# Scan layer and expert tiles: first weights of the last stage into other buffers, and ScalarE's evictions re-ordered

## Chip, cores and metric

One core of a Trainium2 chip runs the whole program. The metric is the device time of one execution in microseconds: the median of three executions of the kernel before is 1581.85 us (1579.13 to 1584.12).

## The reference

`x` is 8 sequences of 512 tokens with 256 features, all float32. A small block computes six modulation vectors for each sequence from `c`. Then:

```
h = layernorm(x) * (1 + ca) + sa
x = x + ga * mamba(h)              # scan layer
h = layernorm(x) * (1 + cb) + sb
x = x + gb * ffn(h)                # 8 experts, 2 for each token

mamba(h):  xi, z = split(rmsnorm(h) @ W_in)          # 512 channels each
           xc = silu(conv(xi)); dt, B, C = split(xc @ W_x)
           dt = softplus(dt @ W_dt + b_dt)
           state = exp(dt * A) * state + dt * xc * B  # 16 states per channel, over 512 tokens
           y = (sum over states of state * C + D * xc) * silu(z)
           return y @ W_out
ffn(h):    scores = h @ Wg; the two best experts of 8, weights by softmax
           out_e = relu((layernorm(h) * gamma_e + beta_e) @ W1_e + b1_e) @ W2_e + b2_e + h
           return the weighted sum of the two
```

`W1` is 256 x 1024 for each expert and `W2` 1024 x 256, 1 MB each in float32. The layernorm ahead of gamma and beta is the same for all experts.

## The kernel before, in words

**The loop.** A body n (0 to 7) runs one sequence through the scan. Its 16 steps s are the 16 states, and each step has four chunks of 128 channels (128 partitions x 512 tokens), so that there are 8 x 16 x 4 = 512 units. For each unit ScalarE computes the decay exp(dt * A) into one of two places in PSUM (`decays`, L1124), GpSimd the input dt * xc * B into a ring of nine tiles `dBu` (L873), and VectorE the scan (L1965), whose result goes over the input. When the four scans of a step are done, TensorE transposes its states in four tiles (`states`, L1477). Two of them VectorE multiplies by C and adds to `y` (L1976), two ScalarE multiplies into `hc` (`times_c`, L1108), and TensorE sums these with the identity (`add_up`, L1486). VectorE is a step ahead of these: it runs scan 0, a product with C, scan 1, scan 2, a product with C, scan 3. A decay waits until the scan two units before has freed its place: this is the "scan ring" (`DA_RING` of 2).

**What rides in the loop.** Between the units of body n lie the preparation of sequence n + 1 (in ScalarE's queue: `norm`, `conv_in`, `softplus_in` and `softplus_exp` at L1091 to 1096, which read the dt product of TensorE at L1466, and `z_in`), and what comes behind the scan for sequence n - 1 (`o_norm` and `o_xhat`, the normalisations of the second half of the layer at L1012; `scores_in`; `top_exp`; `count_in`, L1155, which copies the counts of tokens for each expert that TensorE sums at L1569 to 1573). The order is written out by hand, engine by engine, in one function `body` for each: what stands between `decays(..., (1,))` and `decays(..., (2,))` is run in that place in every body for which its condition holds.

**Tokens by expert.** The output of the second normalisation goes to a table of rows in HBM (`rows_d`, written by GpSimd's indirect transfers, `send_rows`, L791), sorted by expert. A tile is 128 such rows of one expert. Tiles 0 to 11 are computed inside bodies 3 to 7: their W1 and W2 come in halves of 0.5 MB ("pieces") into slots. Slots 0, 1 and 2 lie in `wp` (`expert_pieces` in the profile), slots 3 and 4 are the two halves of `win`, which first held the input weights. TensorE computes them in `tile_h` (L1621) and `tile_y` (L1634), ScalarE evicts the first product with bias and relu in `tile_hin` (L1225), in two halves.

**The last stage.** Tiles 12 to 70 (`BEGIN` is 12, `TILES` is 71) come after the last scan. All eight W2 stay in SBUF (`w2_sb`, in the profile part of `w_sb`, in the places of the ring of inputs, of dt and others), loaded by `all_w2` (L543); W1 comes for each tile into one of two buffers `w1_of` (`late_w1`, L540), the rows by `late_rows` (L530) into one of five. A tile t is: transposes of its rows (`late_x`, L1650), normalisation by gamma and beta with the eviction (`late_xin` on VectorE, L2157), the first product (`first`, 16 products of 128 x 128 by two, L1665), its eviction (`late_hin` on VectorE, L2165), the second product (`second`, L1681), the sum with b2 and the weighting on VectorE (`late_yin`), and a transfer with adding by GpSimd (`late_out`, L860). For tile 12 alone ScalarE does the first eviction (`first_xin`, L1204), with columns of gamma and beta that SyncE loads (`first_columns`). TensorE's order there is: `late_x(12)` and `first(12)` inside step 15 of body 7, the last sums, `y_t`, `first(13)`, `late_x(14)`, `second(12)`, and so on.

**Loads at the hand-over.** SyncE issues nearly all loads in the order of its `epilogue` (L618): tile 11's rows and pieces, small loads, the columns of tile 12, rows of 12, W1 of 12, rows of 13, 14 and 16, W2 of 5 behind the last input product, b2, W2 of 4 behind the last decay, W1 of 13, W2 of 6 and of 7 behind the last transposed state tile (`s_tr`), rows of 15, then W1 and rows of each further tile. A wait in this queue holds everything behind it. Which pieces `late_w1` waits for stands in this condition (tile 12 takes the slots from 3 on, tile 13 the slots 0 and 1):

```
for g in range(4 * BEGIN - 5, 4 * BEGIN):
    if (slot_of(g) >= 3) == (t == BEGIN) and slot_of(g) != 2:
        sp.wait_ge(*piece_read(g))
```

`second(12)` waits for all eight W2 at once (`s_we`), and its PSUM place for the gate of the last sequence.

## Time and profile before

| | |
|---|---|
| median of three executions | 1581.85 us (1579.13 to 1584.12) |
| the profiled execution, its own time | 1585.96 us |
| its span, first to last instruction | 1584.2 us |
| mean granted clock of TensorE | 0.912 |
| busy share of the span: TensorE, VectorE, GpSimd, ScalarE | 84%, 77%, 66%, 49% |
| start of bodies 0, 1, 4, 5, 6, 7 | 66.6, 192.9, 586.5, 716.6, 846.4, 979.3 us |
| last stage | from about 1111 us on, 59 tiles |

All rows below come from this one execution. A row of the windows gives the stretch, its length, the busy time and count of each engine (PE is TensorE's products, PEld its weight loads, DVE VectorE, ACT ScalarE, POOL GpSimd), then the granted clock as a share of full speed, the mean busy share of the 16 DMA engines and GB/s. A row of the timeline gives start and busy time in us, engine (SPq is SyncE's queue), line of the kernel, operation, output and inputs, the number of instructions drawn together, and in brackets how long the engine stood idle before it and what ended that. A row of the waits gives who waited, for whom, the sum in us, how many times, and the longest.

### The profile page before, as it was taken

Reading aid. Unit: us, or ns where it says so; the run is one execution under the profiler, and the core shown is the slowest. Engines: PE = TensorE matmul, PEld = TensorE weight load, DVE = VectorE, ACT = ScalarE, POOL = GpSimd, SP = SyncE. Lnnn points to the kernel's source line nnn. Section 1 sums busy time; section 2 is a strip of 40 time slices with the busy share of each in tenths; the row PEclk is TensorE's granted clock in tenths of the full one; section 3 lists DMA queues with packets and bytes.
Section 4 is the critical chain, followed back from the end, with each engine's and each line's share of the span. In section 5 each row is a group of like instructions: output and inputs, shape, how many; then the busy total and the mean of one; then the engine's idle time right before and its main releaser. Section 6 shows DMA issues by size and latency. Waiting matters only on the chain.

```text
span 1584.2 us, 25969 instructions
## 1 busy us (share of the span) xinstructions
PE 1336.4 (84%) x7986; PEld 1086.1 (69%) x7986; DVE 1219.8 (77%) x2155; ACT 783.9 (49%) x1376; POOL 1044.8 (66%) x942
## 2 busy tenths in 40 slices
PE   3676876876867998788798798869799999999998
PEld 1254564565655776657666576768689989999997
DVE  3798999899899889989989988987355545555554
ACT  2666867767766776786787677666000000000000
POOL 2486778798889789889899878986414352122222
PEclk7787899889889889999999999999899999999999
DMA  6212121223134333244333332674967788766663
GB/s 223 74 48 77 50 54 55 75 92 88 48 100 122 123 114 126 79 143 141 104 107 104 105 111 100 180 235 136 332 179 197 209 241 221 208 194 200 198 193 85
DMA packets 129073, 216.60 MB, mean 137 GB/s; under 512 B 17805, under 2 KB 74649, under 8 KB 128809
## 3 DMA queue, kind: packets, MB, share of 16 engines
q1 hardware_dynamic: 110104, 184.12, 38.0%
q0 software_dynamic: 16064, 27.62, 7.0%
q10 hardware_dynamic: 2768, 3.21, 0.7%
q8 instruction: 66, 1.08, 0.3%
q14 instruction: 71, 0.57, 0.1%
HBM read 178.60 MB, written 37.22 MB: 136 GB/s over the span
## 4 chain that ended last, share of the span: by engine, by line
PE 45%; DVE 18%; POOL 14%; issue 10%; ACT 8%; DMA 3%; SPq 1%; POOLq 0%; DVEq 0%; ACTq 0%
PE psum L1665 13%; PE psum L1681 13%; POOL dBu L873 10%; DVE w_sb L1965 9%; PE psum L1477 6%; DVE y L1976 3%; PE psum L1486 2%; ACT psum L1124 2%; ACT hc L1108 2%; PE psum L1621 1%; PE psum L1466 1%; PE psum L1634 1%; DVE w_sb L1946 1%; DVE xc L1946 1%; DMA w_sb<-in_W 1%
## 5 line engine op out<-in xcount | busy, mean ns | idle before, releaser
L873 POOL TENSOR_TENSOR dBu<-w_sb,brep 128x512 f32<-128x512 f32 x512 | 645.6, 1325 | 42.1 <-issue 18.1
L1965 DVE TENSOR_TENSOR_SCAN w_sb<-psum,dBu 128x512 f32<-128x512 f32 x512 | 611.6, 1210 | 77.5 <-ACT psum L1124 54.6
L1477 PE MATMUL psum<-ident,w_sb 128*128 128x128 f32 x2048 | 316.8, 305 | 116.8 <-DVE y L1976 66.8
L1124 ACT ACTIVATE psum<-w_sb,aneg 128x512 f32<-128x512 f32 x512 | 347.4, 692 | 134.3 <-DVE w_sb L1965 131.4
L1477 PEld LDWEIGHTS psum<-ident,w_sb 128*128 128x128 f32 x2048 | 262.0, 157 | 192.5 <-DVE y L1976 106.1
L860 POOL DMA_INDIRECT out<-dBu,token x59 | 92.2, 1563 | 305.4 <-DMA out<-dBu,token 200.8
L1108 ACT ACTIVATE hc<-psum,ct 128x512 f32<-128x512 f32 x256 | 174.7, 682 | 124.8 <-PE psum L1477 96.6
L1486 PE MATMUL psum<-ident,hc 128*128 128x128 f32 x1024 | 173.7, 302 | 36.2 <-ACT hc L1108 28.8
L1486 PEld LDWEIGHTS psum<-ident,hc 128*128 128x128 f32 x1024 | 135.0, 156 | 81.9 <-ACT hc L1108 53.8
L1976 DVE SCALAR_TENSOR_TENSOR y<-psum,ct,y 128x512 f32<-128x512 f32 x240 | 174.5, 727 | 13.6 <-PE psum L1477 13.1
L1665 PE MATMUL psum<-xn,expert_pieces 128*128 128x128 f32 x928 | 111.4, 280 | 8.2 <-issue 8.2
L1665 PE MATMUL psum<-xgT,win 128*128 128x128 f32 x960 | 113.8, 278 | 1.9 <-issue 1.9
L1665 PEld LDWEIGHTS psum<-xn,expert_pieces 128*128 128x128 f32 x928 | 108.8, 196 | 8.4 <-issue 8.4
L1665 PEld LDWEIGHTS psum<-xgT,win 128*128 128x128 f32 x960 | 111.3, 194 | 2.1 <-issue 2.1
L1681 PE MATMUL psum<-w_sb,xnT 128*128 x480 | 108.7, 379 | 1.4 <-DMA w_sb<-in_W 1.4
L1681 PE MATMUL psum<-w_sb,hmod 128*128 x464 | 105.2, 380 | 4.3 <-issue 4.3
L2165 DVE TENSOR_SCALAR hmod<-psum,b_sb 128x128 f32<-128x128 f32 x232 | 62.7, 343 | 54.1 <-PE psum L1665 47.8
L2165 DVE TENSOR_SCALAR xnT<-psum,b_sb 128x128 f32<-128x128 f32 x240 | 64.8, 343 | 48.0 <-PE psum L1665 47.1
L1681 PEld LDWEIGHTS psum<-w_sb,xnT 128*128 128x128 f32 x480 | 89.0, 190 | 12.5 <-issue 1.6
L1681 PEld LDWEIGHTS psum<-w_sb,hmod 128*128 128x128 f32 x464 | 85.9, 190 | 15.4 <-issue 4.9
L1433 PE MATMUL psum<-xnT,win 128*128 128x512 f32 x112 | 58.3, 636 | 21.1 <-DVE xc L1946 10.9
L791 POOL DMA_INDIRECT rows_d<-xrow,slots x64 | 64.0, 1000 | 16.6 <-issue 14.2
(265 smaller groups left out, 1745.1 us busy)
## 6 DMA issues: line engine op xcount, KB each, us to landing
brep<-b_d SPq DMA_DIRECT2D x128, 256.0 KB, 5.4
win<-in_W SPq DMA_DIRECT2D x30, 1024.0 KB
expert_pieces<-in_W SPq DMA_DIRECT2D x29, 1024.0 KB
expert_pieces<-in_W SPq DMA_DIRECT2D x42, 512.0 KB, 5.3
dBu<-rows_d SPq DMA_DIRECT2D x35, 257.0 KB
w_sb<-in_W SPq DMA_DIRECT2D x8, 1024.0 KB
xg<-rows_d SPq DMA_DIRECT2D x22, 257.0 KB, 2.8
h_d<-hmod SPq DMA_DIRECT2D x8, 512.0 KB, 3.5
```

The lines of the kernel that those rows point to most:

```text
L791: pool.indirect_dma_start(rows_d, bass.IndirectOffsetOnAxis(ap=slots[:, k * TI + i:k * TI + i + 1], axis=0), xrow[:, i, :], None).then_inc ...
L860: pool.indirect_dma_start(out, bass.IndirectOffsetOnAxis(ap=token[:, i % XR:i % XR + 1], axis=0), ysl[:, i % YR, :], None, bounds_check=NT ...
L873: nc.gpsimd.tensor_tensor(dBu[:, i % RING, :], u[p][:, c, :], brep[:, s % 4, :], ALU.mult).then_inc(s_dBu, 1)
L1108: nc.scalar.activation(hc[:, k, :], T[:, 1, :], ACT.Copy, scale=ct[:, p, DT + k, s:s + 1]).then_inc(s_hc, 1)
L1124: nc.scalar.activation(dA[:, i % DA_RING, :], dt[p][:, c, :], ACT.Exp, scale=aneg[:, c, s:s + 1]).then_inc(s_dA, 1)
L1477: last = nc.tensor.transpose(T[:, i // DT, c * P:(c + 1) * P], hs[s % 2][:, c, i * P:(i + 1) * P], ident[:, :])
L1486: last = nc.tensor.matmul(YT[:, DT + k, c * P:(c + 1) * P], hc[:, k, c * P:(c + 1) * P], ident[:, :], start=(s == 0 and c == 0), stop=(s = ...
L1665: last = nc.tensor.matmul(hl(t)[:, f, :], w1_of[t % 2][:, k, f * P:(f + 1) * P], xgT_of[t % 2][:, k, :], start=(k == 0), stop=(k == DC - 1))
L1681: last = nc.tensor.matmul(PS[:, 6 + t % 2, 0:D], hT_late[t % 2][:, k, :], w2_sb[:, bass.ds(e, 1), k, :].rearrange("p a d -> p (a d)"), sta ...
L1965: nc.vector.tensor_tensor_scan(hs[s % 2][:, c, :], dA[:, i % DA_RING, :], dBu[:, (n * UNITS + i) % RING, :], 0.0, ALU.mult, ALU.add).then_ ...
L1976: ins = nc.vector.scalar_tensor_tensor(y[p][:, i, :], T[:, 0, :], c_s, y[p][:, i, :], ALU.mult, ALU.add)
L2165: last = nc.vector.tensor_scalar(hT_late[t % 2][:, f, :], hl(t)[:, f, :], b1_sb[:, bass.ds(e * FC + f, 1)], 0.0, ALU.add, ALU.max)
```

## The change

It has three parts.

1. *Loads.* `w1_of` is turned: W1 of tile 12 goes to slots 1 and 2 of `wp`, W1 of tile 13 to `win`, and `late_w1` waits for the last readers of these. In SyncE's epilogue W1 of tile 12 goes ahead of its rows; the rows of 13, 14 and 16 go behind W2 of expert 5 and b2; W2 of 6 waits for the 508th transposed state tile (`NB * UNITS - TI`, `s_tr`) and not for the 512th, the last; gamma and beta columns of tile 13 and the b1 column of tile 12 are loaded too.
2. *First tiles.* ScalarE, not VectorE, evicts tile 12's first product (`first_hin`) and normalises tile 13 (`first_xin`). The first product of tile 12 is issued in two halves, behind the first sum of step 15 and behind `y_t`.
3. *ScalarE's order in the body.* Tile evictions, `o_xhat`, `count_in` and the exponential of softplus chunk 0 (a step later than before) stand between decays 0 and 1, where they stood behind decay 1 or 2; `softplus_in` of chunk 0 stands behind decay 2 of step 11, where it stood ahead of it; `o_norm` of step 8 is one group of four ahead of decay 3, not two groups of two on either side of it; `rank_in`, `times_c`, `norm` and `norm_t` keep their places.

The diff, cut to its changed lines, one line around each:

```diff
 xgT_of = [xgT[:, :, :], xn[:, 2, :].rearrange("p (k t) -> p k t", t=P)]
-w1_of = [win[:, :, :], wp[:, 0:2, :]]
+w1_of = [wp[:, 1:3, :], win[:, :, :]]
 b2_sb = brep[:, :, :].rearrange("p s l -> p (s l)").rearrange("p (e d) -> p e d", d=D)
...
             for g in range(4 * BEGIN - 5, 4 * BEGIN):
-                if (slot_of(g) >= 3) == (t == BEGIN) and slot_of(g) != 2:
+                if slot_of(g) in ((1, 2) if t == BEGIN else (3, 4)):
                     sp.wait_ge(*piece_read(g))
...
         after(sp, s_th, 2 * t - 2)
+        if t == BEGIN:
+            sp.dma_start(cols[:, t % 2, 0:FC], b1[:, bass.ds(e * FC, FC)]).then_inc(s_cl[t % 2], 16)
         sp.dma_start(cols[:, t % 2, FC:FC + DC], gamma[:, bass.ds(e * DC, DC)]).then_inc(s_cl[t % 2], 16)
...
         first_columns(BEGIN)
+        late_w1(BEGIN)
         late_rows(BEGIN)
-        late_w1(BEGIN)
-        for t in (BEGIN + 1, BEGIN + 2, BEGIN + 4):
-            late_rows(t)
         sp.wait_ge(s_dBu, NB * UNITS)
...
         sp.dma_start(b2_sb, b2.to_broadcast([P, E * D])).then_inc(s_b2, 16)
+        for t in (BEGIN + 1, BEGIN + 2, BEGIN + 4):
+            late_rows(t)
         sp.wait_ge(s_dA, NB * UNITS)
...
         late_w1(BEGIN + 1)
+        first_columns(BEGIN + 1)
+        sp.wait_ge(s_tr, NB * UNITS - TI)
+        all_w2(6)
         sp.wait_ge(s_tr, NB * UNITS)
-        all_w2(6)
         all_w2(7)
...
         act.wait_ge(s_txp, t + 1)
-        act.wait_ge(s_cl[r], 48 * (t // 2) + 32)
-        act.wait_ge(s_thp, 2 * t)
+        act.wait_ge(s_cl[r], 48 * (t // 2) + (48 if t == BEGIN else 32))
+        if t == BEGIN:
+            act.wait_ge(s_thp, 2 * t)
         for k in range(DC):
...
         last.then_inc(s_txt, 1)
+
+    def first_hin(t):
+        r = t % 2
+        act.wait_ge(s_thp, 2 * t + 2)
+        act.wait_ge(s_typ, t - 1)
+        for f in range(FC):
+            last = nc.scalar.activation(hT_late[r][:, f, :], hl(t)[:, f, :], ACT.Relu, bias=cols[:, r, f:f + 1])
+        last.then_inc(s_th, 2)
...
         for s in range(NS):
-            decays(n, p, s, (0, 1), has_o)
-            if n in (3, 7) and s == 0:
-                rank_in(n // 4, XB)
-            times_c_before(n, p, s, 0, has_o)
+            decays(n, p, s, (0,), has_o)
             if 4 <= n <= 6 and s == 0:
                 tile_hin(t - 1, 0)
-            if has_p and s == 1:
-                norm(n + 1, (0, 1))
-            if has_p and s == 3:
-                norm_t(n + 1, 1)
             if n >= 3 and s == 8:
...
                 tile_id(t if n < 7 else LATE + 1)
-            if has_p and s == 11:
-                softplus_in(n + 1, 1 - p, 0, not has_o)
+            if has_p and s == 12:
+                softplus_exp(n + 1, 1 - p, 0)
+            if has_o and s in (13, 14):
+                o_xhat(n - 1, (2 * s - 26, 2 * s - 25))
+            if has_o and s == 13:
+                count_in(n - 1)
+            decays(n, p, s, (1,), has_o)
+            if n in (3, 7) and s == 0:
+                rank_in(n // 4, XB)
+            times_c_before(n, p, s, 0, has_o)
+            if has_p and s == 1:
+                norm(n + 1, (0, 1))
+            if has_p and s == 3:
+                norm_t(n + 1, 1)
             if has_p and s == 12:
...
                 softplus_exp(n + 1, 1 - p, 3)
-            if has_o and s in (13, 14):
-                o_xhat(n - 1, (2 * s - 26, 2 * s - 25))
             if has_p and s == 15:
...
             if has_o and s == 8:
-                o_norm(n - 1, (0, 1))
+                o_norm(n - 1, range(TI))
             if has_p and s == 11:
-                softplus_exp(n + 1, 1 - p, 0)
+                softplus_in(n + 1, 1 - p, 0, not has_o)
             if n == 7 and s == 11:
...
                 tile_hin(LATE + 2, 1)
-            if has_o and s == 13:
-                count_in(n - 1)
             if has_p and s == 13:
...
             decays(n, p, s, (3,), has_o)
-            if has_o and s == 8:
-                o_norm(n - 1, (2, 3))
             if has_p and s == 9:
...
         times_c(NB - 1, 1, NS - 1, 1)
+        first_xin(BEGIN + 1)
+        first_hin(BEGIN)
         load_gate(NB - 1)
...
-    def first(t):
+    def first(t, half=None):
         i = t - BEGIN
-        pe.wait_ge(s_txt, t + 1)
-        pe.wait_ge(s_w1[t % 2], 16 * (i // 2 + 1))
-        if i == 0:
-            pe.wait_ge(s_scan, NB * UNITS)
-        elif i == 1:
-            pe.wait_ge(s_hc, 2 * NS * NB)
-        else:
-            pe.wait_ge(s_th, 2 * (t - 2) + 2)
-        for f in range(FC):
+        if half != 1:
+            pe.wait_ge(s_txt, t + 1)
+            pe.wait_ge(s_w1[t % 2], 16 * (i // 2 + 1))
+            if i == 0:
+                pe.wait_ge(s_scan, NB * UNITS)
+            elif i == 1:
+                pe.wait_ge(s_hc, 2 * NS * NB)
+            else:
+                pe.wait_ge(s_th, 2 * (t - 2) + 2)
+        for f in range(FC) if half is None else range(half * FC // 2, (half + 1) * FC // 2):
             for k in range(DC):
...
                                         start=(k == 0), stop=(k == DC - 1))
-        last.then_inc(s_thp, 2)
+        last.then_inc(s_thp, 2 if half is None else 1)
...
             states(n, s, 3)
-            if n == 7 and s == 15:
-                first(BEGIN)
             if has_o and s == 0:
...
                 add_up(n, s, 0)
+            if n == 7 and s == 15:
+                first(BEGIN, 0)
             if n == 7 and s == 7:
...
         y_t(NB - 1)
+        first(BEGIN, 1)
         first(BEGIN + 1)
...
         dve.wait_ge(s_small, 48)
-        late_xin(BEGIN + 1)
         o_skip(NB - 1, 1)
-        late_hin(BEGIN)
         late_xin(BEGIN + 2)
+        dve.wait_ge(s_th, 2 * BEGIN + 2)
         late_hin(BEGIN + 1)
```

## Rows read from the trace of the kernel before

**Rows 1.** Windows: body 5 and the last stage (columns as said above).

```profile
716.60:846.40 129.80, 111.52 (x640) 85.42 (x640) 120.68 (x165) 97.67 (x173) 117.33 (x103) 0.92 0.37 113
...
1139.00:1584.00 445.00, 432.98 (x2989) 403.93 (x2987) 233.21 (x790) 7.25 (x18) 128.09 (x108) 1.00 0.69 193
```

**Rows 2.** Waits from 58 to 1107 us: who waits for whom, us, count, longest.

```profile
DVE w_sb L1965 <- ACT psum L1124: 54.6, 56, 4.3
```

**Rows 3.** Windows at the hand-over, same columns.

```profile
1098.00:1106.00 8.00, 7.53 (x54) 6.44 (x53) 5.88 (x6) 5.61 (x13) 0.00 (x0) 1.00 0.13 18
...
1128.00:1132.00 4.00, 4.00 (x21) 4.00 (x20) 0.00 (x0) 0.00 (x0) 1.45 (x2) 0.50 1.08 378
```

**Rows 4.** Timeline of TensorE at the hand-over.

```profile
1096.76 0.83 PE L1621 MATMUL psum<-xgT,expert_pieces 128*128 128x128 f32 x6
...
1103.45 2.00 PE L1634 MATMUL psum<-win,hmod 128*128 128x256 f32 x8
...
1127.06 6.75 PE L1665 MATMUL psum<-xn,expert_pieces 128*128 128x128 f32 x32 [8.21 <-issue]
...
1135.41 3.72 PE L1681 MATMUL psum<-w_sb,xnT 128*128 x16 [1.39 <-DMA w_sb<-in_W]
...
1150.75 3.74 PE L1665 MATMUL psum<-xn,expert_pieces 128*128 128x128 f32 x32
```

**Rows 5.** Timeline of SyncE's queue at the hand-over: issues of loads.

```profile
1106.25 0.39 SPq L540 DMA_DIRECT2D win<-in_W  x1
...
1113.02 4.38 SPq L540 DMA_DIRECT2D expert_pieces<-in_W  x1
...
1117.44 5.44 SPq L543 DMA_DIRECT2D w_sb<-in_W  x2
```

**Rows 6.** Timeline of GpSimd and VectorE at the hand-over.

```profile
1124.88 1.02 POOL L791 DMA_INDIRECT rows_d<-xrow,slots  x1 [0.16 <-issue]
...
1134.20 0.73 DVE L2157 TENSOR_SCALAR xgT<-psum,gam,bet 128x128 f32<-128x128 f32 x2 [10.52 <-PE psum L1650]
```

**Rows 7.** Timeline of body 4, steps 8 and 9, all engines.

```profile
651.10 2.35 PE L1621 MATMUL psum<-xgT,expert_pieces 128*128 128x128 f32 x16
...
653.26 0.69 ACT L1124 ACTIVATE psum<-w_sb,aneg 128x512 f32<-128x512 f32 x1 [1.08 <-DVE w_sb L1965]
...
655.39 1.13 ACT L1225 ACTIVATE gT<-psum,cols 128x128 f32<-128x128 f32 x4
...
657.00 1.11 ACT L1012 ACTIVATE xf<-x,nb,rs 128x256 f32<-128x256 f32 x2
...
657.14 1.22 DVE L1965 TENSOR_TENSOR_SCAN w_sb<-psum,dBu 128x512 f32<-128x512 f32 x1 [0.89 <-ACT psum L1124]
...
664.32 1.22 DVE L1965 TENSOR_TENSOR_SCAN w_sb<-psum,dBu 128x512 f32<-128x512 f32 x1 [0.38 <-ACT psum L1124]
```

**Rows 8.** Timeline of body 4, step 11, all engines.

```profile
675.24 1.09 PE L1477 MATMUL psum<-ident,w_sb 128*128 128x128 f32 x8 [0.92 <-DVE w_sb L1965]
...
679.11 0.69 ACT L1091 ACTIVATE w_sb<-psum,bdt 128x512 f32<-128x512 f32 x1 [2.05 <-PE psum L1466]
...
680.99 1.22 DVE L1965 TENSOR_TENSOR_SCAN w_sb<-psum,dBu 128x512 f32<-128x512 f32 x1 [2.67 <-ACT psum L1124]
...
684.47 1.83 PE L1477 MATMUL psum<-ident,w_sb 128*128 128x128 f32 x8
...
686.33 0.69 ACT L1108 ACTIVATE hc<-psum,ct 128x512 f32<-128x512 f32 x1 [1.06 <-PE psum L1477]
```

**Rows 9.** Timeline: body 4 step 13, body 3 step 14, body 5 step 0.

```profile
692.12 1.32 ACT L1124 ACTIVATE psum<-w_sb,aneg 128x512 f32<-128x512 f32 x2
...
693.41 1.04 PE L1573 MATMUL psum<-mask,ones 128*128 128x32 f32 x8
...
575.57 1.22 DVE L1965 TENSOR_TENSOR_SCAN w_sb<-psum,dBu 128x512 f32<-128x512 f32 x1 [0.83 <-ACT psum L1124]
...
720.19 1.22 DVE L1965 TENSOR_TENSOR_SCAN w_sb<-psum,dBu 128x512 f32<-128x512 f32 x1 [0.63 <-ACT psum L1124]
```

## The prediction

> **What bounds the kernel now.** I read the windows by body first, then waits, then timelines. In a steady body of 130 us VectorE is busy for 93% and the others for less [rows 1]; after 1139 us TensorE is busy for 97% of the stretch at full clock [rows 1]. So the loop hangs mostly on VectorE, the tiles on TensorE, and whatever lets the tiles start sooner shortens the kernel one for one as long as they stay packed. The waits of the loop have one tall row: scans wait 54.6 us in 56 places for ScalarE's decays [rows 2]. The hand-over between the two parts is a third regime: the DMA engines move 18 GB/s until 1106 us, then run full, as at 378 GB/s with all 16 busy from 1128 to 1132 us [rows 3], while TensorE stands 8.21 us before tile 13's first product and 1.39 us before tile 12's second one, which a load of W2 releases [rows 4]. The loads go out from 1106.25 us on, and SyncE stands up to 5.44 us in an issue, since the queue is full [rows 5].
>
> **The hand-over, part by part.** *First weights to the pieces.* `late_w1(12)` now goes to pieces 1 and 2, not to `win`. `win` comes free with the W2 half product that ends at 1103.45 + 2.00 = 1105.45 us; the issue follows 0.80 us later. Piece 2 is free when the first-half product of tile 11 ends, 1096.76 + 0.83 = 1097.59 us [rows 4]. With the same 0.8 us the issue stands at 1098.4: **7.85 us earlier**, into the idle DMA stretch [rows 3]. The gather of tile 12 (issued at 1093.6 us before) falls behind it; its 257 KB add 0.26/0.38 = 0.7 us to the packed stretch. It is needed by TensorE only at 1108 us, so nothing else waits. The three other gathers move behind W2 of expert 5 and b2: on SyncE they cost an issue each, beside a queue that already has 3 MB to do. W2 of 4 needs the last decay, `win` (for tile 13) is free at 1105.45, W2 of 6 may now go one step earlier, W2 of 7 as before; at about 3 us for each MB these buffers are free before their turn comes, so I see no bubble. Three small column loads more (gamma and beta of tile 13, b1 of tile 12) cost SyncE what any issue costs, 0.39 us [rows 5], and the DMA engines nothing beside a megabyte. Behind the new wait for the 508th transposed tile only W2 of 6 and 7 are queued, and both needed it anyway.
>
> The packed stretch, which before ended for tile 12 with W2 at 1135.28 us, thus ends 7.85 - 0.7 = **7.15 us** earlier if every byte stays ahead of it. GpSimd's four row scatters (from 1124.88 us, 257 KB each, 1.05 MB in all [rows 6]) lay ahead of that end. They hang on the gate of the last batch, which hangs on tile 12's first product, and this I place at 1120.2 us, only 4.7 us sooner. So they drop partly or wholly out of the way: at most 1.05/0.38 = 2.8 us more. **Between 7.15 and 9.9 us; I take 8.5**, the middle.
>
> The Trainium skill (DMA: Bandwidth & Descriptors, Issuing engines are not separate DMA queues) says that transfers started by GpSimd and by SyncE run on the same 16 engines and interleave. By that rule the scatters always take their share, and the term would be the lower end.
>
> *TensorE's own path.* First product of tile 12: one half after the first sum of step 15, at 1110.2, at full clock 3.74/2 = 1.9 us [rows 4]; a sum, tile 13's transposes and `y_t`, about 2 us, then the other half: 1116. Tile 13's first product needs W1 of 13, in front of which nothing is added or taken but tile 12's gather: 1127.06 - 7.15 = 1119.9. It takes 3.74 us, and the transposes and VectorE's 0.73 us [rows 6] with their hand-overs take, as before, from the product's end at 1133.8 to 1135.3 us, so the second product may start at 1125.2. If the clock is at its lower level, as when that product took 6.75 us after the idle 8.21 us [rows 4], it is 1128.2. W2 lands at 1135.3 - 8.5 = 1126.8. The two are abreast; DMA still decides, with little in hand.
>
> *ScalarE in the first two tiles.* `first_hin(12)`: eight pieces, priced by its own four-piece evictions, 1.13 us [rows 7], 2.3 us, done by 1118.5; `first_xin(13)`, two pieces, under 1 us. VectorE loses as much work. Nobody waits for either at that time: cost and gain nothing, the cover being the wait for W2. If that cover went, TensorE would still have tile 13's product before it. What follows on ScalarE waits for GpSimd's part of the last batch in any case.
>
> **The re-ordered evictions, bodies 1 to 7.** The work is the same; only its place in ScalarE's queue changes, from between decays 1 and 2 to between 0 and 1, where ScalarE idles 1.08 us for the scan ring [rows 7]. Step by step, in body 4:
> - *Steps 8 and 9.* Tile evictions move up: the 0.89 us in front of scan 2 goes. But `o_norm` now has four pieces (two pairs of 1.11 us) ahead of decay 3, not two, and the last scan of the step gets later by some 0.6 us. Step 9 gets back the 0.38 us at its scan 2 [rows 7]. Net **0.3 us**, four bodies with tiles: 1.2 us.
> - *Step 11.* The tallest wait, 2.67 us: ScalarE stands 2.05 us for a dt product before decay 2 [rows 8]. Decay 2 now goes first and scan 2 starts 2.7 us sooner. Yet from 675.24 us TensorE works without a hole to 686.30 us, and ScalarE's next product with C starts at 686.33 when the transposes from 684.47 end [rows 8]; from there ScalarE is busy to the next step. The scans come early to a meeting that does not move: **0**. Late next: the same TensorE chain.
> - *Step 13.* `count_in` moves ahead of decay 1. The counts on TensorE end at 693.41 + 1.04 = 694.45 us; ScalarE would be there at 693.95 (decay 0, started at 692.12, 0.7, then two normalisations, 1.10) and stands 0.5 us, with decays 1 to 3 behind it, and VectorE's sum of dt behind those [rows 9]. **-0.5 us**, six bodies: -3.0 us.
> - *Step 14.* In bodies 1 and 3 the normalisations stood before decay 2 and cost 0.83 us [rows 9]; they move away: +1.6 us.
> - *Step 0 of bodies 4 to 6* loses its wait of 0.63 us [rows 9] and gives that back, since TensorE has a transpose or product of every chunk to do there without a pause: 0. The other steps keep their order.
>
> Sum 1.2 - 3.0 + 1.6 = **-0.2 us**, nothing. Bounds: no more than the 54.6 us of [rows 2], since no other wait is touched; below, the 0.5 us of step 13 turned into the 2.05 us of step 11's wait, 1.55 us more in six bodies: -9.5 us. Most of the tall waits end on TensorE's products, so I stay near zero.
>
> **Sum.** 8.5 - 0.2 = 8.3 us off the profiled execution's 1585.96 us (span 1584.2): 1577.7. That execution lies 4.1 us over the median of the three runs, 1581.85; against the median **1573.6 us**. About 0.3% (4.7 us) is what a measurement of this kernel can tell from no change.
>
> **Rivals.**
> *A. The waits in front of scan 2 are on the path.* Then each steady body gains what its moved evictions cost: 0.63 + 0.89 + 0.38 + 2.67 = 4.6 us, four bodies, 18 us; with the hand-over 26.5: **1555 us**. For it: VectorE is the busiest engine of the loop. Against: the packed TensorE stretch of [rows 8]. Chance 0.11.
> *B. The clock eats the hand-over.* TensorE fell to 0.5 of its clock after its idle stretch and was there still from 1128 to 1132 us [rows 3]. If tile 13's first product (6.75 for 3.74 us) and the following second one (3.72 doubled) run at the 1.2 GHz level, that is 3.0 + 3.7 us on a path that is abreast of DMA: of 8.5 us about 3 are left, **1578.5 us**, no change that can be told. For it: one idle stretch still comes before tile 13. Against: it is 3 us, not 8.21. Chance 0.12.
> The Trainium skill (TensorE: Matmul & The Clock Gate, HAM oscillation) has a load's wait throttle the array so that the next work starts cold; in this trace it did, and by the rule any remaining wait makes B true.
> *C. Slower: ScalarE waits for TensorE with decay 1 behind it.* The moved evictions (tile 9's in body 7, the counts, the tiles' second halves) read products; where one is late, decays 1 to 3 and all scans are late. The price is that of step 11, 2.67 us in each of seven bodies, 18.7 us: 1581.85 - 8.5 + 18.7 = **1592 us**. It decides from 1.9 us per body on (8.5 + 4.7 over 7). For it: step 13. Against: step 8's product ends at 653.45, just as the scan ring opens at 653.26 [rows 7]. Chance 0.07.
>
> **Numbers.** Forecast 0.70, its own range 1567 to 1579. A 0.11, B 0.12, C 0.07. The range for 8 in 10 runs from 1562, part of the way to A, to 1580, which takes B in and leaves C out. Faster: 0.70 x 0.95 + 0.11 = 0.78; the rest of the forecast and B with a little of C 0.16; slower 0.06.
>
> **What would show it.** Right: DMA at over 350 GB/s from 1100 us; tile 13's first product at about 1120 and tile 12's second at about 1127; TensorE packed after it as before; scan 2 of step 11 without its 2.67 us, yet ScalarE's product with C still released by TensorE at the same place in the body; a new wait of ScalarE before the counts' copy; bodies of 130 us as before. Wrong: bodies shorter by over 2 us (A), a second product of 7 us (B), decay 1 waiting with TensorE as releaser at several steps and bodies of 132 us (C), or a hole of TensorE before tile 14's first product, whose W1 comes last in the packed stretch.

## The result and the profile after

The changed kernel takes **1564.13 us** (median of four executions, 1562.95 to 1566.44) against 1580.69 us for the kernel before (four executions beside it, 1579.13 to 1584.12): a ratio of 0.9884, 95% interval 0.9868 to 0.9900. That is 16.6 to 18.3 us, twice the 8.3 us forecast. The time lies inside the range for 8 in 10 (1562 to 1580), but outside the forecast's own (1567 to 1579), about midway between the forecast (1573.6) and rival A (1555). The profiled execution took 1562.95 us, its span is 1561.1 us. Two executions further below, one of `steps13_14_only` (1667.49 us) and one of `after_again` (1960.96 us), ran at a mean granted clock of 0.81 and 0.64 and are in no ratio.

The page of the profile of the changed kernel, its head and its first part:

```profile
span 1561.1 us, 25964 instructions
## 1 busy us (share of the span) xinstructions
PE 1319.3 (85%) x7986; PEld 1072.1 (69%) x7986; DVE 1219.1 (78%) x2145; ACT 786.6 (50%) x1386; POOL 1045.2 (67%) x942
```

VectorE, ScalarE and GpSimd do the same work as before. TensorE's busy time fell from 1336.4 us to 1319.3 us with the same 7986 products: it ran less of its time at the low clock.

The windows of the changed kernel (columns as in [rows 1]): body 5, the last stage from tile 14's first product on, and two stretches of the hand-over.

```profile
707.20:834.30 127.10, 109.45 (x648) 83.47 (x646) 121.02 (x164) 97.75 (x174) 117.31 (x103) 0.95 0.37 115
...
1114.56:1561.00 446.44, 434.54 (x2987) 404.94 (x2986) 233.01 (x790) 7.25 (x18) 129.87 (x109) 0.99 0.68 193
...
1082.00:1090.00 8.00, 7.53 (x53) 6.47 (x52) 6.25 (x7) 4.89 (x11) 0.00 (x0) 1.00 0.95 303
1104.00:1108.00 4.00, 4.00 (x23) 4.00 (x24) 0.00 (x0) 1.99 (x8) 2.94 (x3) 0.63 1.10 369
```

Body 5 is 2.7 us shorter than in [rows 1] (its stretch holds 648 products, there 640, so nothing was left out); VectorE is busy for 95% of it instead of 93%. The DMA engines, at 18 GB/s in the stretch before the last sums in [rows 3], now move 303 GB/s there.

And the waits up to the last scan, with the row that answers to [rows 2]:

```profile
ACT psum L1128 <- DVE w_sb L1981: 114.8, 136, 3.5
...
DVE w_sb L1981 <- ACT psum L1128: 36.2, 51, 4.2
...
ACT gT L1238 <- PE psum L1635: 11.4, 9, 2.4
```

The scans wait 18.4 us less for decays. The last of the three rows is ScalarE waiting for TensorE in a tile's eviction with decay 1 behind it.

**Where the time went.** Lengths of the bodies, from the first scan of one to the first scan of the next, and from the last scan to the end of the program. The columns before are the trace shown, a second trace of the same kernel and that of `tail_only` below, whose bodies are those of before; the columns after are the changed kernel twice, and `order_only` and `after_loads_only`, whose bodies are the changed ones:

```
body        before                 changed                        mean gain
0        126.2 123.7 126.2     123.3 126.0 123.3 123.5              1.4
1        128.9 126.5 128.8     124.2 124.3 124.2 124.3              3.8
2        127.7 128.0 127.7     125.7 125.8 125.7 125.7              2.1
3        137.0 132.5 137.0     136.0 136.0 136.0 136.0             -0.5
4        130.1 129.7 130.2     130.6 130.6 130.6 130.6             -0.6
5        129.8 129.8 129.8     127.2 127.1 127.1 127.1              2.7
6        132.9 132.9 132.9     130.0 130.0 130.0 130.0              2.9
7        126.0 124.9 124.4     124.2 124.3 123.6 123.6              1.2
loop    1038.7 1027.9 1037.1  1021.2 1024.1 1020.6 1020.8         12.9
rest     478.8  478.8  (470.7)  472.5  472.8 (482.5) (473.1)        6.2
```

(The values of the rest in brackets have another hand-over than their column and are left out of its mean.) So two thirds of the gain are in the loop, where the forecast had -0.2 us, and one third behind it, where it had 8.5. These are differences of traces, one execution each, and their sum of 19.1 us is above the 16.6 to 18.3 us of the medians.

The 6.2 us of the rest are low. The rest differs between executions too: over all seven traces with the loads of before it is 478.8 to 482.8 us (mean 480.7), and the two of the kernel before are the shortest of them; over the seven with the new loads it is 470.7 to 473.9 us (mean 472.5). So the hand-over is worth about 8.2 us, near the 8.5 forecast, and no trace of one kind reaches one of the other.

### The profile page after: what moved, and what is told of

The parts are those of the page before. It is cut to its first block, busy times and chain, and to the rows that moved or that the text cites. A ratio compares the mean times of both kernels' runs of the same rounds, so it can differ in the third digit from the quotient of the medians.

```text
span 1561.1 us, 25964 instructions
## 1 busy us (share of the span) xinstructions
PE 1319.3 (85%) x7986; PEld 1072.1 (69%) x7986; DVE 1219.1 (78%) x2145; ACT 786.6 (50%) x1386; POOL 1045.2 (67%) x942
## 4 chain that ended last, share of the span: by engine, by line
PE 52%; DVE 19%; issue 9%; ACT 9%; POOL 8%; DMA 1%; SPq 1%; DVEq 0%; POOLq 0%; ACTq 0%
PE psum L1680 13%; PE psum L1696 13%; DVE w_sb L1981 9%; PE psum L1491 8%; POOL dBu L877 6%; DVE y L1992 3%; PE psum L1500 3%; ACT psum L1128 3%; PE psum L1635 2%; ACT hc L1112 2%; PE psum L1457 2%; PE psum L1648 1%; DVE xc L1962 1%; DVE w_sb L1962 1%; PE psum L1480 1%
## 5 line engine op out<-in xcount | busy, mean ns | idle before, releaser
L1491 PE MATMUL psum<-ident,w_sb 128*128 128x128 f32 x2048 | 306.4, 297 | 124.3 <-DVE y L1992 70.5
L1491 PEld LDWEIGHTS psum<-ident,w_sb 128*128 128x128 f32 x2048 | 250.7, 152 | 199.4 <-DVE y L1992 101.7
L1500 PE MATMUL psum<-ident,hc 128*128 128x128 f32 x1024 | 172.5, 300 | 34.4 <-ACT hc L1112 23.9
L1680 PE MATMUL psum<-xn,win 128*128 128x128 f32 x928 | 109.9, 277 | 5.6 <-ACT xn L1215 5.6
L1680 PE MATMUL psum<-xgT,expert_pieces 128*128 128x128 f32 x960 | 112.3, 275 | 0.0
L1680 PEld LDWEIGHTS psum<-xn,win 128*128 128x128 f32 x928 | 107.3, 194 | 5.8 <-ACT xn L1215 5.8
L1680 PEld LDWEIGHTS psum<-xgT,expert_pieces 128*128 128x128 f32 x960 | 109.7, 192 | 0.2
L795 POOL DMA_INDIRECT rows_d<-xrow,slots x64 | 64.0, 1000 | 16.6 <-issue 13.7
```

The source lines that it names most:

```text
L795: pool.indirect_dma_start(rows_d, bass.IndirectOffsetOnAxis(ap=slots[:, k * TI + i:k * TI + i + 1], axis=0), xrow[:, i, :], None).then_inc ...
L1491: last = nc.tensor.transpose(T[:, i // DT, c * P:(c + 1) * P], hs[s % 2][:, c, i * P:(i + 1) * P], ident[:, :])
L1500: last = nc.tensor.matmul(YT[:, DT + k, c * P:(c + 1) * P], hc[:, k, c * P:(c + 1) * P], ident[:, :], start=(s == 0 and c == 0), stop=(s = ...
L1680: last = nc.tensor.matmul(hl(t)[:, f, :], w1_of[t % 2][:, k, f * P:(f + 1) * P], xgT_of[t % 2][:, k, :], start=(k == 0), stop=(k == DC - 1))
```

## The experiments

### Hand-over alone

`tail_only` is the kernel before with parts 1 and 2 of the change:

```diff
-        w1_of = [win[:, :, :], wp[:, 0:2, :]]
+        w1_of = [wp[:, 1:3, :], win[:, :, :]]
...
+                late_w1(BEGIN)
                 late_rows(BEGIN)
-                late_w1(BEGIN)
...
+                first_xin(BEGIN + 1)
+                first_hin(BEGIN)
```

> The kernel before with the hand-over part alone: first weights into the pieces, ScalarE in the first two tiles; ScalarE's order in the bodies as before. Theory P (the forecast's own split, hand-over 8.5 us): 7 to 9 us faster than before, about 1573, and the rest of the 17 us is the order of evictions. Theory H (the whole gain is made at the hand-over): 15 to 17 us faster, about 1565. In the trace both want the last scan at 1105 us as before; P wants the first second-layer product of the last stage 22 us after the last scan (before: 30.1), H wants it earlier still or the last stage shorter than 448.8 us.

Measured: 1576.32 us (12 executions) against 1581.12 (23), ratio 0.9958 (0.9938 to 0.9979), so 6.6 us (3.3 to 9.8). The last scan ends at 1104.1 us, tile 12's second product 22.7 us behind it instead of 30.1. That is near theory P's 7 to 9 us, a little under them, and its interval takes them in; H falls.

### Order of the evictions alone

`order_only` is the kernel before with part 3:

```diff
-                    decays(n, p, s, (0, 1), has_o)
+                    decays(n, p, s, (0,), has_o)
...
+                    decays(n, p, s, (1,), has_o)
```

> The kernel before with the re-ordered evictions alone; loads and first tiles as before. Theory P (the forecast: the order gives nothing): within 2 us of before, 1581. Theory O (the waits in front of scan 2 and the clock behind them were on the path): 8 to 11 us faster, about 1571, the last scan at 1088 to 1095 us of the trace instead of 1105, and the wait of scan 2 in step 11 gone with the following step starting over 2 us earlier in most bodies.

Measured: 1569.70 us (6 executions), ratio 0.9905 (0.9870 to 0.9940): 11.4 us between the medians, 15.0 by the ratio. The last scan ends at 1087.6 us. Theory O holds, with a gain at or above its upper end and the last scan a little ahead of its place, and the forecast's "nothing" falls. The two parts, 6.6 and 11 to 15 us, make the whole within their intervals. In this trace the loop is 14.0 us shorter than the mean of the three before, and the stage behind it 3.7 us longer (482.5 us, within the spread of the rest told above), with a second product of tile 12 that starts 32.0 us behind the last scan, not 30.1.

### Step 11 alone

```diff
-                    if has_p and s == 11:
-                        softplus_in(n + 1, 1 - p, 0, not has_o)
+                    if has_p and s == 12:
+                        softplus_exp(n + 1, 1 - p, 0)
...
                     if has_p and s == 11:
-                        softplus_exp(n + 1, 1 - p, 0)
+                        softplus_in(n + 1, 1 - p, 0, not has_o)
```

(The first place is ahead of decay 2, the exponential's new one between decays 0 and 1, the last behind decay 2.)

> The kernel before with one move alone: softplus_in of chunk 0 behind decay 2 of step 11, its exponential between decays 0 and 1 of step 12. Theory O1 (the tall wait of 2.67 us was on the path, since TensorE's stretch behind it was slow by its clock and not full of work): 2.3 to 2.7 us in each of bodies 3 to 6 and about 3 in body 1, 8 to 12 us faster, 1571. Theory P (the meeting with TensorE does not move): within 2 us, 1581. Theory O2 (the gain is spread over steps 8, 9, 13 and 14): 2 to 4 us faster.

Measured: 1575.27 us (12 executions), ratio 0.9961 (0.9941 to 0.9982): 6.2 us, interval 2.8 to 9.3. That excludes P. It lies between O2 and O1, and the interval touches both. The trace says why it is less than O1: the wait in front of scan 2 (2.67 us in bodies 3 to 6 before) is gone in every body that had it, and bodies 1, 2 and 3 are 3.5, 2.1 and 1.4 us shorter. But body 5 is only 0.9 us shorter (its step 8 takes 9.05 us instead of 7.71), and bodies 4 and 6 are 0.4 and 1.2 us **longer**. In those two TensorE's clock falls in step 11. The windows over steps 11 and 12 (from scan 0 of step 11 to scan 0 of step 13) of this kernel, body 4 and body 5:

```profile
665.32:684.86 19.54, 18.08 (x92) 12.83 (x92) 16.65 (x36) 15.88 (x28) 18.33 (x14) 0.83 0.44 132
...
796.94:812.93 15.99, 13.96 (x83) 9.31 (x83) 14.90 (x35) 14.06 (x25) 14.83 (x12) 1.00 0.51 158
```

The same two steps last 19.54 us at a mean clock of 0.83 and 15.99 us at 1.00. In the kernel before, with its wait, body 5:

```profile
805.04:822.80 17.76, 16.66 (x82) 11.51 (x82) 14.56 (x36) 14.06 (x25) 14.80 (x12) 0.81 0.47 142
```

In the changed kernel both happen, first body 4 and then body 5:

```profile
664.27:684.91 20.64, 19.56 (x92) 13.40 (x92) 16.45 (x35) 14.91 (x26) 18.04 (x14) 0.75 0.42 125
...
794.76:810.69 15.93, 13.91 (x83) 9.25 (x83) 14.89 (x35) 14.00 (x26) 14.54 (x12) 1.00 0.50 158
```

So without the wait the two steps win 1.8 us if the clock holds, and lose 1.8 to 2.9 us if it falls. Over the whole body the difference is smaller, since step 13 is shorter where the clock fell in step 11 (8.50 us against 9.67).

### The kernel before once more

No edit.

> The kernel before as it is, for a second trace: how far its bodies differ between two executions. Theory S (the bodies repeat): lengths of bodies 4 to 6 within 0.3 us of 130.1, 129.8 and 132.9 us, and the low-clock stretch of TensorE in step 11 in each of them. Theory R (the clock falls by chance): some of these bodies 2 to 3 us shorter, without that stretch.

Measured: one execution of 1575.98 us. Bodies 5 and 6 repeat to 0.1 us (129.8, 132.9), body 4 within 0.5 (129.7 instead of 130.1, outside theory S's 0.3), and step 11's low clock was there in all three. Theory S holds for them otherwise, and R's bodies without that stretch did not come. Bodies 1 and 3 do not repeat: 126.5 and 132.5 us instead of 128.9 and 137.0. These two make 6.9 of the 10.8 us between the loops of the two traces.

### Filling TensorE's idle places ahead of step 11

```diff
                         tile_h(t, 1)
+                        add_zeros(1)
...
+                    if has_p and has_o and s == 8:
+                        add_zeros(1)
                     if has_p and s == 8:
                         c_t(n + 1)
...
                         add_up(n, s, 1)
+                    if has_p and has_o and s == 9:
+                        add_zeros(2)
```

> The kernel before, ScalarE's order untouched, with products of zeros (of 512 columns, added into the accumulating sum) in TensorE's idle places ahead of step 11: one behind tile_h of step 7, one ahead of c_t of step 8, two behind the last sum of step 9. Theory K (what costs the time in steps 11 and 12 is TensorE's clock, which falls there to 0.5 for 6.8 us; its chain and not the wait of scan 2 sets the pace): with less idle time ahead the clock holds in step 11, bodies 4 to 6 get 2 to 3 us shorter each though scan 2 still waits over 2 us, and the whole is 5 to 10 us faster, about 1574. Theory W (the wait of scan 2 itself is the cost, 2.67 us): no body gets shorter, within 2 us of before or a little slower, 1581 to 1584. If the clock falls in step 11 all the same, the run tells nothing between the two.

Measured: 1584.73 us (12 executions), ratio 1.0021 (1.0006 to 1.0036): 3 us slower. The clock did hold in step 11 of bodies 4 to 6, and they took 130.8, 129.9 and 133.0 us, none shorter. (The larger changes of this trace are elsewhere: body 2 took 133.1 us, 5.3 more, and body 7 120.0 us, 5.1 less, with the low clock in other places.) Body 5, steps 11 and 12 of this kernel:

```profile
807.07:825.41 18.34, 14.91 (x87) 9.63 (x85) 15.16 (x36) 14.83 (x26) 14.81 (x12) 1.00 0.45 138
```

At full clock throughout the two steps take 18.34 us, no less than the 17.76 us at a clock of 0.81, and the scan still waits (2.74 us; the profile names GpSimd's input there, but decay 2 ends at 813.37 us, 0.03 us ahead of the scan). Even with the 0.58 us by which step 11 is longer than before taken off, nothing is won. Theory W holds: as long as the wait is there, TensorE's clock behind it costs nothing in these steps. Theory K, that TensorE's chain behind the wait sets the pace of this stretch, falls. It was the core of the forecast's zero.

### Steps 8 and 9 alone, steps 13 and 14 alone

```diff
+                    if n >= 3 and s == 8:
+                        tile_hin(t if n < 7 else LATE + 1, 0)
...
+                        o_norm(n - 1, range(TI))
```

(The edit moves the tile evictions of step 0 too.)

> The kernel before with the tile evictions of steps 0, 8 and 9 between decays 0 and 1, and o_norm of step 8 as one group of four; steps 11 to 14 as before. The forecast priced this at 0.3 us in each body with tiles, 1.2 us in all: 1580. From the trace of the changed kernel, where step 10 of body 5 starts 1.0 us earlier than before: 1 us a body, 4 us, 1577. If the gain of 0.5 to 1 us is given back before the body ends, since step 11's wait meets TensorE all the same: 0.

Measured: 1578.99 us (12 executions), ratio 0.9990 (0.9975 to 1.0005), an interval that takes in 0, the forecast's 1.2 us and, just, the 4 us. Steps 8 and 9 of body 5 take 14.62 us instead of 15.71, and step 10 0.15 us more, so 0.9 us are won; then step 12 takes 8.48 us instead of 7.59, since the low clock lasts longer, and body 5 takes 129.7 us instead of 129.8. In this trace its gain is given back.

```diff
+                    if has_o and s in (13, 14):
+                        o_xhat(n - 1, (2 * s - 26, 2 * s - 25))
+                    if has_o and s == 13:
+                        count_in(n - 1)
                     decays(n, p, s, (1,), has_o)
```

> The kernel before with o_xhat and count_in alone between decays 0 and 1 (steps 13 and 14). The forecast: 0.5 us lost at step 13 in six bodies, 0.83 us gained at step 14 in bodies 1 and 3: -1.4 us, 1582.5. Rival: the counts are late by more, as behind an untouched step 11 ScalarE comes to them later: no loss at step 13, gain at step 14 alone, 1 to 2 us faster, 1579.5.

Measured: 1581.81 us (12 executions), ratio 0.9991 (0.9971 to 1.0011), nothing that can be told: the interval takes in both the forecast's loss and the rival's gain. In body 5 step 13 takes 9.76 us instead of 9.37, step 14 8.02 instead of 8.43, so the loss at step 13 is there and step 14 gives it back.

### The changed kernel with another order of loads

```diff
-                sp.dma_start(b2_sb, b2.to_broadcast([P, E * D])).then_inc(s_b2, 16)
...
                     late_rows(t)
+                first_columns(BEGIN + 1)
...
                 late_w1(BEGIN + 1)
-                first_columns(BEGIN + 1)
...
                 all_w2(7)
+                sp.dma_start(b2_sb, b2.to_broadcast([P, E * D])).then_inc(s_b2, 16)
```

> The changed kernel with SyncE's queue in another order: gamma and beta of tile 13 ahead of W2 of expert 4, and the 1 MB of b2 behind W2 of 7. In the changed kernel tile 13's first product starts 15.4 us after the last scan, 1.4 us behind the landing of its W1, and the last stage's first second product 22.1 us after it, 1.1 us behind the landing of W2 of 7. Theory D (bytes of the packed stretch decide): without 1 MB ahead W1 of 13 and W2 of 7 land 2.5 to 2.8 us earlier and TensorE follows, 3 to 3.5 us faster than the changed kernel, about 1561 against its 1564 and 0.986 of before. Theory T (TensorE's own path, its clock low after the wait, decides): under 1 us of it is seen. Rival: b2 now lands after the first late_yin needs it, and the gain goes into that wait.

Measured: 1559.81 us (6 executions, 1548.39 to 1565.06), ratio 0.9863 (0.9831 to 0.9896). The interval overlaps that of the changed kernel, so it isn't shown to be faster. TensorE's timeline at its hand-over:

```profile
1096.92 3.81 PE L1680 MATMUL psum<-xn,win 128*128 128x128 f32 x32 [1.58 <-issue]
...
1103.83 5.32 PE L1696 MATMUL psum<-w_sb,xnT 128*128 x16 [2.88 <-DMA w_sb<-in_W]
...
1111.97 3.81 PE L1680 MATMUL psum<-xgT,expert_pieces 128*128 128x128 f32 x32 [2.60 <-DVE xn L2173]
```

The last scan ends at 1085.6 us here. Tile 13's first product starts 11.4 us behind it (changed kernel: 15.4), tile 12's second 18.3 us (22.1): theory D holds so far. But tile 14's first product starts 26.4 us behind it, in the changed kernel 26.0: its W1 comes last in the packed stretch, and all megabytes are ahead of it in either order. (The row names VectorE, but the last record of this W1's landing is at 1111.88 us, 0.09 us ahead of the product and behind VectorE's end.) The gain went into that wait and into a second product at the low clock, 5.32 us for 3.72. In the trace shown the gain comes mostly from the loop: body 4 kept its clock. Whether the other executions owe their 4.3 us of the median to that isn't shown.

```profile
665.15:681.09 15.94, 13.91 (x83) 9.24 (x83) 14.90 (x36) 14.01 (x26) 14.56 (x12) 1.00 0.53 158
```

That is the same code as the body 4 that took 20.64 us for these steps, and the body is 127.8 us long instead of 130.6. The two kernels differ only in loads that SyncE issues behind the last input product, over 400 us later. So the fall in body 4 isn't settled by the program: it differs between executions of the same instructions.

### The changed kernel once more

No edit.

> The changed kernel as it is, timed beside its variants of this call, and a second trace. If the gains are those of the two parts alone (tail_only 0.9958, order_only 0.9905), 0.986 to 0.989 of before. Its bodies 5 and 6 should again be 127.2 and 130.0 us with TensorE's clock held through step 11; if body 4 is again 130.6 us, its clock has fallen in step 11 again, if that fall is missing, 127.8 us.

Measured: 1563.69 us (6 executions), ratio 0.9871 (0.9844 to 0.9899). Bodies 1 to 7 repeat within 0.1 us, body 4 with its fallen clock.

### The changed kernel with the filling

The diff is that of the filling above, on the changed kernel.

> The changed kernel with the products of zeros of before_filler in TensorE's idle places ahead of step 11. There the clock held in bodies 4 to 6 and nothing was won, since scan 2 still waited 2.74 us and step 11 became 0.58 us longer. Theory B (both are needed: no wait in front of scan 2, and the clock held): body 4's steps 11 and 12, 20.6 us in the changed kernel with its clock fallen, take 16 to 16.6 us here, bodies 5 and 6, where the clock held anyway, get up to 0.6 us longer each; the whole within 2 us of the changed kernel, 1562 to 1566. Theory W2 (the wait alone is the cost, the clock is nothing): no body below its length in the changed kernel, 3 us slower.

Measured: 1570.72 us (6 executions), ratio 0.9920 (0.9893 to 0.9948), 7 us slower than the changed kernel. In body 4 the clock fell in step 11 all the same (for 6.8 us, not 10.2), and its steps 11 and 12 took 20.1 us; in body 6, where it had held, it now fell, and the body took 133.3 us. In body 5 it held, and the fillers cost 1.4 us. Body 2 took 129.3 us, 3.6 more than changed, and bodies 3 and 7 were shorter (134.9 and 121.7 us), with the low clock in other places. So this run doesn't decide between its theories. It shows that these fillers don't keep the clock up in every body, and that body 6 loses its gain when the clock falls.

### The changed kernel without ScalarE's part in the first tiles

```diff
-                first_xin(BEGIN + 1)
-                first_hin(BEGIN)
...
+                late_xin(BEGIN + 1)
                 o_skip(NB - 1, 1)
+                late_hin(BEGIN)
...
-                first(BEGIN, 1)
```

> The changed kernel without ScalarE's part in the first tiles: tile 12's first product whole and where it was, its eviction and tile 13's normalisation on VectorE, no columns for tile 13; loads and the order in the bodies as in the changed kernel. Theory D (the forecast: DMA decides, ScalarE's part costs and gains nothing): tile 12's second product 21.5 to 22.5 us after the last scan as in the changed kernel (22.1), 1564. Theory T (TensorE's path decides once the loads are early): it starts 24 to 27 us after the last scan, 2 to 5 us slower than the changed kernel. Rival: faster by about 1 us, since tile 13's first product no longer waits for its beta column, 1.4 us.

Measured: 1563.66 us (6 executions), ratio 0.9879 (0.9854 to 0.9903), the changed kernel's time. TensorE at the hand-over of this kernel, whose last scan ends at 1088.2 us:

```profile
1103.00 5.81 PE L1665 MATMUL psum<-xn,win 128*128 128x128 f32 x32 [4.72 <-issue]
...
1110.39 3.72 PE L1681 MATMUL psum<-w_sb,xnT 128*128 x16 [1.35 <-DVE xgT L2157]
```

The second product starts 22.2 us behind the last scan. Theory D holds: the loads are the whole of the hand-over's gain, within what the two medians tell. The rival's 1 us doesn't show: tile 13's first product starts 14.8 us behind the last scan, 0.6 us sooner than in the changed kernel, and the second product doesn't.

### The changed kernel with steps 0, 8 and 9 as before

The diff is that of `steps8_9_only`, taken back.

> The changed kernel with the tile evictions of steps 0, 8 and 9 and o_norm of step 8 where they were before; steps 11 to 14, loads and first tiles as changed. In the changed kernel steps 8 and 9 of body 5 take 14.56 us against 15.71 before and step 10 0.15 us more. Theory A (that gain is kept once the wait of step 11 is gone): bodies 5 and 6 are about 1 us longer than in the changed kernel, 128.2 and 131.0 us, and the whole 3 to 4 us slower, 0.990 of before against 0.988. Theory N (it is given back within the body, as it was where steps 8 and 9 alone were changed: 0.999): bodies and the whole as in the changed kernel, 0.988. If the clock falls in step 11 of body 5 or 6, which it did not in the changed kernel, these bodies take 3 to 4 us more, whatever the theory.

Measured: 1565.21 us (6 executions), ratio 0.9896 (0.9863 to 0.9929), within 2 us of the changed kernel. Bodies 5 and 6 took 129.9 and 133.5 us, 2.7 and 3.5 us more than changed, with the clock fallen in step 11 of both, and body 1 127.3 us, 3.1 us more; against that body 3 took 134.1 us, body 0 122.9 and body 7 119.7 us (136.0, 123.3 and 124.2). So A's and N's bodies can't be told apart here, and neither theory is shown. What the run does show is that in this trace the clock fell in step 11 of other bodies.

## Why the prediction was wrong

**The step that failed is "the scans come early to a meeting that does not move: 0"**, the price of step 11. It was put at nothing; `step11_only` measured 6.2 us for it (2.8 to 9.3), the largest part of the 8.3 us that the forecast fell short. The forecast took TensorE's stretch of [rows 8] for a chain that sets the end of the step. Nobody in VectorE's queue waited for it: once scan 2 had its decay at 680.99 us, scan 3 and step 12's scan 0 followed without a wait. VectorE's wait was therefore on the path, and `before_filler` shows it from the other side: TensorE at full clock, the wait in place, nothing won. In the changed kernel, body 5, the timeline of ScalarE and then of VectorE:

```profile
798.58 0.69 ACT L1095 ACTIVATE w_sb<-psum,bdt 128x512 f32<-128x512 f32 x1 [1.47 <-PE psum L1480]
...
800.45 1.22 DVE L1981 TENSOR_TENSOR_SCAN w_sb<-psum,dBu 128x512 f32<-128x512 f32 x1 [0.54 <-ACT psum L1128]
```

ScalarE still waits for the dt product (1.47 us, 2.05 in [rows 8]), but decay 2 has gone ahead of it; the wait now falls before scan 3 and is 0.54 us. Step 11 takes 8.35 us instead of 10.17: of the 2.67 us of the wait 1.8 us are won.

**A second reading lay in the same rows and was missed.** The eight transposes of states at 675.24 us took 1.09 us, the eight at 684.47 us took 1.83 us [rows 8]. That is not more work but the low clock, as the granted clock of two stretches of that trace says, 0.50 and 1.00:

```profile
679.30:686.00 6.70, 6.70 (x26) 4.84 (x24) 4.94 (x22) 5.84 (x10) 3.91 (x5) 0.50 1.02 342
675.24:679.00 3.76, 3.76 (x27) 2.98 (x27) 3.07 (x4) 1.35 (x2) 3.59 (x4) 1.00 0.32 35
```

In the changed kernel, body 4, with the clock fallen:

```profile
664.22 1.09 PE L1491 MATMUL psum<-ident,w_sb 128*128 128x128 f32 x8 [0.86 <-DVE w_sb L1981]
665.15 2.07 PE L1543 MATMUL psum<-wg,gT 128*128 128x8 f32 x16
667.15 2.07 PE L1480 MATMUL psum<-xn,wdt_and_b_rows 64*128 64x512 f32 x2
669.15 1.97 PE L1491 MATMUL psum<-ident,w_sb 128*128 128x128 f32 x8
```

and body 5, where it held:

```profile
797.41 1.12 PE L1480 MATMUL psum<-xn,wdt_and_b_rows 64*128 64x512 f32 x2
798.47 1.09 PE L1491 MATMUL psum<-ident,w_sb 128*128 128x128 f32 x8
799.49 1.12 PE L1480 MATMUL psum<-xn,wdt_and_b_rows 64*128 64x512 f32 x2
```

With the wait gone and the clock low, TensorE's chain does become the pace, as the forecast had it: VectorE then waits for the transposes in body 4.

```profile
670.31 0.75 DVE L1992 SCALAR_TENSOR_TENSOR y<-psum,ct,y 128x512 f32<-128x512 f32 x1 [1.73 <-PE psum L1491]
```

So, steps 8 and 9 included, bodies 5 and 6 gained 2.7 and 2.9 us, and bodies 3 and 4, where the clock fell, lost 0.5 and 0.6 us. Over bodies 1 to 7 the order gave 11.5 us in the loop (the table's gains ahead of rounding), where the sum had -0.2. By step, from the starts of the scans in the same seven traces: steps 11 and 12 gave 6.0 us, steps 8 to 10 3.6 (1.5 of them in body 7), steps 13 and 14 4.0 (3.4 of them in body 3), step 0 cost 3.0 (2.4 of them in body 3), the others gave 0.9. Alone, only the share of step 11 was clear of the noise. This was rival A's mechanism at less than its price (4.6 us in a body; measured 2.9 at most in bodies 3 to 6). Body 0 has 1.4 us more, but it varies by 2.5 to 2.7 us with either order, so that isn't shown to be the change's.

**The other terms of the order.**
- Steps 8 and 9: forecast 0.3 us a body, though its own three amounts, 0.89 - 0.6 + 0.38, make 0.67; 15.71 us became 14.56 in body 5, step 10 lengthened by 0.15, so 1.0 us. The term was too small. Alone it was given back in body 5 (`steps8_9_only`).
- Step 13: the forecast had ScalarE stand 0.5 us ahead of the counts. It stands 0.65 us:

```profile
811.97 0.20 ACT L1159 ACTIVATE cnt_sb<-psum 128x40 f32<-128x40 f32 x1 [0.65 <-PE psum L1587]
```

  The step lengthens by 0.30 us in body 5, and step 14 gets 0.24 of it back. The mechanism was right, the loss of 3.0 us was not: nearly all of it came back within the body.
- Step 14: forecast 1.6 us in bodies 1 and 3. The step was 0.9 and 1.7 us shorter than in the trace of the forecast (9.06 and 9.72 us became 8.17 and 7.98), but `before_again`, with the old order, has 7.97 and 8.43 us. So most of this wait was that execution's and not the order's.
- Step 0: forecast 0 in bodies 4 to 6. Steps 0 and 1 of body 5 take 16.77 us instead of 16.28, those of body 6 16.28 in both. In body 3, of which the forecast said nothing, step 0 takes 9.62 us instead of 7.23, the first of these two rows, at the low clock throughout; the second is the kernel before:

```profile
440.60:450.22 9.62, 9.03 (x40) 8.01 (x40) 5.98 (x7) 4.00 (x7) 9.05 (x10) 0.50 0.23 82
...
449.43:456.66 7.23, 5.64 (x40) 4.61 (x40) 5.88 (x8) 3.94 (x7) 6.66 (x8) 0.81 0.31 109
```

  `step11_only` has the 9.6 us too. So the loss of body 3 lies in step 0 as well as in steps 11 and 12.
- Rival C, a product not ready with decay 1 behind it, came true in body 7, step 8:

```profile
1029.10 1.14 ACT L1238 ACTIVATE hmod<-psum,cols 128x128 f32<-128x128 f32 x4 [5.65 <-PE psum L1635]
...
1030.86 2.41 DVE L1981 TENSOR_TENSOR_SCAN w_sb<-psum,dBu 128x512 f32<-128x512 f32 x2 [4.21 <-ACT psum L1128]
```

  Whether it cost anything isn't shown: steps 8 and 9 of that body take 19.35 us, before 20.81, but 21.16 and 20.07 us in the second traces of the two kernels. The 18.7 us that C was priced at did not come.

**The hand-over was right in mechanism and near in size.** SyncE's issues and TensorE in the changed kernel, whose last scan ends at 1088.6 us (before: 1105.3):

```profile
1081.68 0.39 SPq L540 DMA_DIRECT2D expert_pieces<-in_W  x1
...
1090.01 3.07 SPq L540 DMA_DIRECT2D win<-in_W  x1
```

```profile
1103.99 5.23 PE L1680 MATMUL psum<-xn,win 128*128 128x128 f32 x32 [5.60 <-ACT xn L1215]
...
1110.70 3.72 PE L1696 MATMUL psum<-w_sb,xnT 128*128 x16 [1.26 <-DVE xgT L2173]
...
1157.91 5.40 PE L1696 MATMUL psum<-w_sb,hmod 128*128 x16 [1.91 <-issue]
```

W1 of tile 12 is issued 6.9 us ahead of the last scan, before 0.95 us behind it: 7.87 us earlier, forecast 7.85. Tile 13's first product comes 15.4 us behind the last scan, where the forecast's 1119.9 us meant 14.6. Tile 12's second product comes 22.1 us behind it instead of 30.1: 8.0 us of the 8.5 forecast (in `tail_only`, with the old bodies, 22.7). The end came only 6.3 us nearer to the last scan in these two traces (8.2 us between the means of all fourteen). In the trace shown some of that went into TensorE: a hole of 1.91 us ahead of 1157.91 us and a product of 5.40 us behind it (its neighbours take 3.62). In the second trace it is tile 13's first product, which took 6.68 us, with the second 23.9 us behind the last scan:

```profile
1106.30 6.68 PE L1680 MATMUL psum<-xn,win 128*128 128x128 f32 x32 [5.73 <-ACT xn L1215]
```

That is rival B's mechanism at 1.5 to 2.9 us in one product (5.23 and 6.68 against 3.74 us), not the 5.5 it was priced at. One cost was called nothing and was something: the three small loads more. ScalarE stood for the beta column of tile 13 until 1103.13 us:

```profile
1103.13 0.81 ACT L1215 ACTIVATE xn<-psum,cols 128x128 f32<-128x128 f32 x2 [9.56 <-DMA cols<-in_beta]
```

W1 of tile 13 had landed at 1102.63 us, so the product was 1.4 us late. `after_loads_only`, without these loads, shows that it changed nothing at the second product.

The Trainium skill (TensorE: Matmul & The Clock Gate, HAM oscillation) has the array throttled after a wait for a load, so that the next work starts cold. At the hand-over the traces agree, 5.23 and 6.68 us for a product that takes 3.74 us in [rows 4]. In step 11 the fall came with no wait for a load, and the longest idle place of TensorE in the 8 us ahead of it was 0.86 to 1.01 us (eight falls in the traces of the kernel before, the changed one and `step11_only`).

**What stays open.** Why the clock falls in step 11 in one body and not in the next. The same code kept it in body 4 of one execution and lost it in four others. Under other orders and with fillers it fell in other bodies, in one trace of each kernel. No run here controls it, so 3.6 to 4.7 us (19.54 and 20.64 against 15.93 to 15.99 us for steps 11 and 12), of which 2.8 us are left over the whole of body 4 (130.6 against 127.8), hang on something that these runs don't explain. Open too is what made the order's 11 to 15 us out of step 11's 6.2: the parts alone (6.2, 1.6 and 1.4 us) make 9.2, and the intervals don't tell that from the whole. A shift of the whole loop in time, with nothing else changed, wasn't tried.

## What to carry to other kernels

Before a wait is called free because "the engine behind it is packed", look at who stands still at the end of the stretch: if the waiting engine's next instructions follow without a gap, its wait is on the path, unless the packed engine is so slow that it takes over once the wait is gone (as in body 4 at the low clock). Compare the duration of the same group of products in two places before calling a TensorE stretch full of work: 1.09 and 1.9 us for the same eight are a clock, not a load, and a chain at half clock can absorb a gain that the same chain at full clock passes on. And a part of 1 us a body can't be judged by its time alone: the move in steps 8 and 9 gave 1.6 us alone and cost 1 to 2 us when taken back, both within the noise, and in both traces other bodies changed by more than that. Compare such a part step by step, in more than one trace, with the granted clock beside it.

## What the runs showed of the hardware

- TensorE's clock fell to its lower level (a granted clock of 0.5, 1.2 GHz) three to seven times in every body of the kernels before and changed (two traces of each), with TensorE 70 to 86% busy over a body. Whether it fell in step 11 or not differed for the same instructions: body 4 of the changed kernel and of the one with b2 last start 0.3 us apart (576.6 and 576.9 us), and it fell in the first only. Body 4 of `after_loads_only` starts at 576.9 us too, and there it fell.
- Step lengths repeat closely between executions when the clock is the same (step 11 of bodies 5 and 6: 8.35 and 8.34, 8.34 and 8.35 us in two traces), and of the 10.8 us between the loops of two traces of the kernel before 9.4 are in bodies 0, 1 and 3, where the stretches at the low clock differ.
- Fillers on TensorE in places that looked idle weren't free: four products of 0.59 us each cost 1.4 us in body 5 of the changed kernel, where the clock had held without them.
